# Last group's tail in parts of one, one and two images, bands with tap rows only, first tiles 24 units later

## The reference

```
x = x + L0(gn(x))   # focal modulation: linear, 3 depthwise convs (3, 5, 7), gates, linear, LayerNorm, linear
x = x + L1(gn(x))   # LayerNorm, fp8-quantised MLP 64 -> 512 -> 64
x = x + L2(gn(x))   # circular 7x7 depthwise convs by FFT, gates, 8-step scan, linear
x = x + L3(gn(x))   # deformable 3x3 conv: offsets by a conv, 4-corner gather at 9 taps, linear
```

## Time and profile before

| | |
|---|---|
| median of 3 runs | 5436.56 us (5429.32 to 5450.64) |
| profiled execution | 5432.24 us, its span 5430.4 us |
| mean granted TensorE clock | 0.678 of full speed |
| busy share of DVE, PE, POOL, ACT | 61, 56, 53, 32% |
| bytes moved | 763 MB, mean 141 GB/s |

### The profile page before, as it was taken

The page is one execution under the profiler, slowest core; times in us unless marked ns, Lnnn a source line. Parts: engine busy times, 40 slices in busy tenths (PEclk is TensorE's granted clock), DMA queues, the critical chain, the costliest instruction groups (busy, mean ns, idle before and its releaser), DMA issues. The chain is left out here.

```text
span 5430.4 us, 92964 instructions
## 1 busy us (share of the span) xinstructions
PE 3017.6 (56%) x39574; PEld 2623.4 (48%) x39574; DVE 3303.5 (61%) x4063; ACT 1729.1 (32%) x3209; POOL 2876.9 (53%) x2614
## 2 busy tenths in 40 slices
PE   2873235669644466559744466569744463455333
PEld 2872135559633365449633365469633353444222
DVE  4347843575678755575678765575788655554333
ACT  1223424622234245421233245421333242232000
POOL 1000000465566665565566765674666766677776
PEclk9965655669767666669667666669766666655555
DMA  6841174569633575559633575569633564654333
GB/s 165 169 97 22 29 139 140 145 149 223 149 97 104 127 199 171 146 141 230 140 90 104 135 190 175 155 150 238 141 106 98 149 182 133 178 171 135 109 106 93
DMA packets 776762, 763.09 MB, mean 141 GB/s; under 512 B 575244, under 2 KB 652460, under 8 KB 771916
## 3 DMA queue, kind: packets, MB, share of 16 engines
q1 hardware_dynamic: 651931, 417.24, 33.3%
q0 software_dynamic: 124416, 339.90, 21.7%
HBM read 637.12 MB, written 136.73 MB: 143 GB/s over the span
## 5 line engine op out<-in xcount | busy, mean ns | idle before, releaser
L2129 POOL DMA_INDIRECT e_gb<-corner_table,e_idx x2592 | 2862.3, 1104 | 2534.1 <-DMA e_cws<-cw_all 1084.0
L2191 DVE TENSOR_TENSOR e_vw<-e_gb,e_pc 128x1024 f32<-128x1024 f32 x576 | 774.3, 1372 | 685.4 <-DMA e_gb<-corner_table,e_idx 663.4
L2157 PE MATMUL e_pv<-shifts,e_vw 128*128 128x128 f32 x2744 | 536.7, 365 | 464.0 <-DVE e_vw L2198 463.8
L2157 PEld LDWEIGHTS e_pv<-shifts,e_vw 128*128 128x128 f32 x2744 | 440.3, 190 | 496.9 <-DVE e_vw L2198 474.6
L488 PE MATMUL e_pw<-wk,e_vt 128*64 128x64 f32 (+1 forms) x2880 | 325.1, 285 | 348.0 <-DVE e_xr L2209 221.2
L488 PEld LDWEIGHTS e_pw<-wk,e_vt 128*64 128x64 f32 (+1 forms) x2880 | 279.7, 192 | 410.1 <-issue 248.6
L502 PE MATMUL b_p<-b_x,b_tt 100*100 100x96 f32 x4096 | 398.2, 259 | 32.7 <-DMA b_tt<-zl_copies 32.7
L2167 ACT ACTIVATE e_vt<-e_pv 128x512 f32<-128x512 f32 x288 | 184.2, 640 | 727.3 <-PE e_pw L2157 726.5
L502 PEld LDWEIGHTS b_p<-b_x,b_tt 100*100 100x100 f32 x4096 | 391.0, 176 | 35.3 <-DMA b_tt<-zl_copies 35.2
L1926 ACT ACTIVATE f_xall<-f_p 64x384 f32<-64x384 f32 (+2 forms) x320 | 301.7, 1056 | 132.6 <-PE f_p L1821 130.3
L2198 DVE TENSOR_TENSOR e_vw<-e_vw 128x1152 f32<-128x1152 f32 x233 | 335.4, 1440 | 8.0
(11 more groups left out here) (309 smaller groups left out, 7094.8 us busy)
## 6 DMA issues: line engine op xcount, KB each, us to landing
b_tt<-zl_copies SPq DMA_DIRECT2D x256, 234.0 KB, 9.5
b_tt<-zl_copies SPq DMA_DIRECT2D x128, 390.0 KB
e_gb<-corner_table,e_idx POOLq DMA_INDIRECT x2592
d_px<-x_halo SPq DMA_DIRECT2D x32, 1152.0 KB
corner_table<-f_xn SPq DMA_DIRECT2D x128, 288.0 KB
f_xall<-xpad SPq DMA_DIRECT2D x10, 2400.0 KB, 16.1
x_halo<-d_xo SPq DMA_DIRECT2D x128, 144.0 KB
d_wd<-wd_rows SPq DMA_DIRECT2D x8, 1890.0 KB
```

The source lines that it names most:

```text
L2129: nc.gpsimd.indirect_dma_start(self.gb[k][:, 4 * q:4 * q + 4, :].rearrange("p a c -> p (a c)"), None, T.table[m], off)\
L2157: last = nc.tensor.matmul(dst, vw[:, a, 2 * q:2 * q + nq, :].rearrange("p k c -> p (k c)"), T.ident[:, :], start=(a == 0), stop=(a == n - ...
L2191: v.tensor_tensor(dst, self.gb[k][:, 4 * k0:4 * k1, :].rearrange("p (k a) c -> p k a c", a=4), bc(w, [128, k1 - k0, 4, C], 3), ALU.mult).t ...
```

## The change

- `PARTS`: group 3's D and F run over parts of one, one and two images. `StageF.steps(1)` is a list of its own. Places that took a part of two or more for granted (`load_x(1)`, `k < 2`, `load(0), load(1)`) ask for `P.n`; `P.base // 2` becomes `P.seen[...]`, a count of the images in each buffer; `StageF.act` gets one more place for a tile's copy.
- `StageB.load` brings KS0 rows instead of ND0; `zeros` writes the other rows of both buffers, once a group, on DVE in stage A's step k = 1, p = 0; `first` waits for that.
- `plan`: the first tile is due 24 units after the placement; the third group's spacing (tiles 144 to 215) is made 70/72 of a unit smaller, the last group's is 12.0 instead of 9.0.

```diff
     def load(self, sp, l, q):
         T = self.T
+        n = KS0[l] * PITCH
         for hi in range(2):
-            src = bass.AP(T.zlw.tensor, T.zlw.offset + ORG0[l] - PITCH * hi + 4 * q * W * ZL0,
-                          [[ZL0 - 1, W], [W * ZL0, 4], [1, LB[l]]])
-            dst = halves(self.tt[:, q % 2, OB[l]:OB[l] + 4 * LB[l]])[hi].rearrange("p (c t) -> p c t", c=4)
+            skip = (2 * RD0[l] - KS0[l] // 2 + hi) * PITCH
+            src = bass.AP(T.zlw.tensor, T.zlw.offset + ORG0[l] - PITCH * hi + skip + 4 * q * W * ZL0,
+                          [[ZL0 - 1, W], [W * ZL0, 4], [1, n]])
+            dst = halves(self.tt[:, q % 2, OB[l]:OB[l] + 4 * LB[l]])[hi].rearrange("p (c t) -> p c t", c=4)[:, :, skip:skip + n]
             sp.dma_start(dst, src).then_inc(self.t_in[l][q % 2], 16)
+    def zeros(self, dve, G):
+        for q in range(2):
+            for l in range(3):
+                lead = (2 * RD0[l] - KS0[l] // 2 + 1) * PITCH
+                n = ND0[l] * PITCH - lead - (KS0[l] - 1) * PITCH
+                assert n == lead
+                t = self.tt[:, q, OB[l]:OB[l] + 4 * LB[l]]
+                ap = apv(t, 0, [list(t.ap[0]), [LB[l], 4], [LB[l] - lead, 2], [1, lead]])
+                last = self.nc.vector.memset(ap, 0.0)
+        last.then_inc(self.S.b_zero, 1)
+
     def first(self, sp, G):
         n = 2 * (OB[2] + 4 * LB[2])
+        sp.wait_ge(self.S.b_zero, G + 1)
...
         if k == 1:
             self.st.enter(sp, P.G, P.stage)
-            load_x(1)
+            if P.n > 1:
+                load_x(1)
...
-                pe.wait_ge(self.p_in[m % 2], 48 * (P.base // 2 + m // 2 + 1))
+                pe.wait_ge(self.p_in[m % 2], 48 * (P.seen[m % 2] + m // 2 + 1))
...
     def steps(n):
+        if n == 1:
+            return [10, 14, 6] + [12, 16, 6] + [12, 10, 8] + [1]
         return [10, 14, 6] + [16, 22, 6] + [22, 26, 6] * (n - 2) + [16, 20, 6] + [12, 10, 8] + [1]
...
-PARTS = parts_of([(NI,)] * (NGRP - 1) + [(2, 2)])
+PARTS = parts_of([(NI,)] * (NGRP - 1) + [(1, 1, 2)])
...
-    spaces = [(b - a) / (NI * J) for a, b in zip(starts, starts[1:])] + [9.0]
+    spaces = [(b - a) / (NI * J) for a, b in zip(starts, starts[1:])] + [12.0]
+    spaces[-2] -= 70.0 / (NI * J)
...
                 if tiles == J * loaded:
-                    due = clock
+                    due = clock + 24.0
```

More of the change, by code:

```diff
@@ L672, in dve @@
             gn.dve_var(dve, link, self.psn, PP, i)
+        if k == 1 and p == 0:
+            self.after.zeros(dve, G)
         if 1 <= k <= NI and p:
@@ L697, in __init__ @@
         self.nc, self.T, self.st = nc, T, st
-        self.S = sems(nc, ctx, "b_t00 b_t01 b_t10 b_t11 b_t20 b_t21 b_gap b_zlw b_halo b_c0 b_c1 b_c2 b_g0 b_g1 b_g2 b_acc b_mean b_ctx b_gt")
+        self.S = sems(nc, ctx, "b_t00 b_t01 b_t10 b_t11 b_t20 b_t21 b_gap b_zero b_zlw b_halo b_c0 b_c1 b_c2 b_g0 b_g1 b_g2 b_acc b_mean b_ctx b_gt")
         S = self.S
@@ L1518, in pe @@
             self.st.enter(pe, P.G, P.stage)
-        if k < 2 and p == 0:
+        if k < min(2, P.n) and p == 0:
             gn.pe_sum(pe, self.psn, NH, gn.of(P, 0, k))
@@ L1555, in square @@
         def square():
-            act.wait_ge(self.x_in[k % 2], 64 * (P.base // 2 + k // 2 + 1))
+            act.wait_ge(self.x_in[k % 2], 64 * (P.seen[k % 2] + k // 2 + 1))
             if m >= 1:
@@ L1618, in sums @@
         def sums():
-            dve.wait_ge(self.x_in[k % 2], 64 * (P.base // 2 + k // 2 + 1))
+            dve.wait_ge(self.x_in[k % 2], 64 * (P.seen[k % 2] + k // 2 + 1))
             gn.dve_sums(dve, NH, xs[:, 3:NR + 3, :], self.sq, gn.of(P, 0, k))
@@ L1769, in sp @@
             self.st.enter(sp, P.G, P.stage + 1)
-            load(0)
-            load(1)
+            for m in range(min(2, P.n)):
+                load(m)
             for u in range(2):
@@ L1963, in act @@
             if mid:
+                if not new and not old:
+                    between()
                 moves(0)
@@ L2004, in dve @@
         if p == 1 and j < P.n:
-            dve.wait_ge(self.x_in[j % 2], 16 * (P.base // 2 + j // 2 + 1))
+            dve.wait_ge(self.x_in[j % 2], 16 * (P.seen[j % 2] + j // 2 + 1))
             for g in range(3):
@@ L2209, in result @@
         v.tensor_tensor(xr, xr, self.pso, ALU.add).then_inc(S.e_res, 1)
-Part = namedtuple("Part", "G first n base turn stage")
+Part = namedtuple("Part", "G first n base turn stage seen")
 def parts_of(sizes):
-    parts, turn = [], 0
+    parts, turn, seen = [], 0, (0, 0)
     for G, group in enumerate(sizes):
@@ L2220, in parts_of @@
         for n in group:
-            parts_of_group.append(Part(G, first, n, G * NI + first, turn, 4 + 2 * len(parts_of_group)))
-            first, turn = first + n, turn + 1
+            parts_of_group.append(Part(G, first, n, G * NI + first, turn, 4 + 2 * len(parts_of_group), seen))
+            first, turn, seen = first + n, turn + 1, (seen[0] + (n + 1) // 2, seen[1] + n // 2)
         parts.append(parts_of_group)
     return parts
-PARTS = parts_of([(NI,)] * (NGRP - 1) + [(2, 2)])
+PARTS = parts_of([(NI,)] * (NGRP - 1) + [(1, 1, 2)])
 def sequence():
```

## The result

The changed kernel takes 5380.24 us (5371.95 to 5390.53, 4 runs) beside 5433.0 us for the kernel before: ratio 0.990, interval 0.987 to 0.993, 1.0% faster. A second comparison gave 0.990 again (0.988 to 0.991). The profiled execution has a span of 5388.8 us, 41.6 less than before's.

A forecast was written before the change was run, and what follows sets the result against it. Trunk bounds until image 12's placement, then GpSimd nearly. Placement 4521 - 60 - 20 + 12 - 67 + 13 = 4399; plus 497 + 8 + 439.5 gives span 5343.5, time 5350 us; 8-in-10 range 5280 to 5412.

The forecast's parts named there:

- The stall of the first tile: F's tail after each group's first placement: TensorE's 24.8 us wait goes; -20 us a group, -60 for three.
- Bands: Stage B: loading only tap rows, 15/22 of the bytes, cuts TensorE's waits for bands; -20 us, range 0 to -40.
- The second part: Last group, image 12's placement to image 13's: 84 us to the first gate, then body, F and tiles; 212 us.
- The third part: Last group, images 14 and 15, up to image 14's placement: head 98, bodies 75, F 100, denser tiles 12; 285 us.
- and 12 for the denser tiles: Third part: 12 us added because tiles 12 units apart come every 10.4 us, under GpSimd's 11.7.
- the +66: Image 12's placement to image 14's: second and third parts together take 497 us instead of 431.
- the -31: Image 14's placement to its first tile: GpSimd is idle, so it starts after 7.9 us instead of 38.5.
- seven more tiles in A to L: Last group's stages A to L take seven tiles moved from D and F, 1.9 us each; +13 us, range 0 to +29.
- the head stalls on gathers: Rival: three tiles in each of two heads cost 16.5 us apiece, +99 us, 5450; chance 0.08.
- The moved stall: Rival: tiles 72 to 78 come due at GpSimd's pace, so F's tail ends where it did; +60, 5410; chance 0.15.
- The quick trunk: Rival: parts two and three run at one us a unit (451), F tails gain 29 us each; 5277, chance 0.2.
- the estimate of 5320: Two new heads: at 358 GB/s from HBM their 6.8 MB take 19 us, some 30 us less in all; not adopted.

The follow-up runs named there:

- late48: `parts22` with the first tile due 48 units after the placement instead of 24 and the third group's tiles closer: 5341 us, 0.981 of the kernel before.
- late72: `parts22` with the first tile due 72 units after the placement instead of 24 and the third group's tiles closer: 5316 us, 0.976 of the kernel before.
- space15: The changed kernel with the last group's tiles 15 units apart instead of 12: 5402 us, 0.991 of the kernel before.
- only_late: The kernel before with only the first tile due 24 units after the placement: 5397 us, 0.991 of the kernel before.
- only_bands: The kernel before with only the bands' tap rows loaded, the zeroing memsets and the wait: 5421 us, 0.995 of the kernel before.
- only_parts: The kernel before with only the parts of one, one and two images and their spacings: 5495 us, 1.009 of the kernel before.
- parts22: The changed kernel with the last group's parts and spacings put back to two and two images; bands and 24 units stay: 5374 us, 0.987 of the kernel before.

## Why the prediction was right, and where its steps were off

The direction held, and 5380 us lies in the range, at 0.6 of the gain forecast. Point by point:

- *The stall of the first tile* was right in place and size: 20 us a group forecast, 18, 25 and 12 measured, and -50 us for this edit alone. That GpSimd's pace would be late next was right too: `late48` and `late72` took more from the same stretch.
- *Bands*: right in kind, half the size. The forecast counted TensorE's waits, 33 us, and took 20. Stage B lost 41. What the waits didn't show is the clock, granted at 0.95 for 0.91, and the smaller idle times between the matmuls. The Trainium skill, "DMA: Bandwidth & Descriptors", Anatomy of one DMA, fits a single DMA of the software path as about 2.0 us plus bytes over 436 GB/s. By it a cut band would save an estimated 0.2 us of its landing; the median landing fell by 4.8 us, so the fit doesn't carry over to these transfers of SP's queue, which share the engines at shares of 0.86 to 1.04. Why the granted clock rose wasn't tried.
- *Zeros*: 3.9 us a group forecast, 3.8 measured (16 memsets of 752 ns and 8 of 405).
- *Part one of one image*: -67 forecast, -61.4 measured.
- *The second part* was 212 us in the forecast and is 211, with 83 us from placement to first gate for 84. That is in part luck: 10 of the 83 are waits for gathers that the forecast put at nothing, and with three tiles fewer `space15` took 187, 8 us a tile. *The third part* was 285 and is 313. Its head took 92 us for 98; its bodies and F took 221 for 187.
- The step that failed is "and 12 for the denser tiles": it was mis-sized, and so was the 1.9 us a tile that the forecast took from stages with a tile every 17 us. That VectorE waits 26 us for gathers in the 47 us ahead of image 14's placement doesn't show it, since the kernel before has 27 us there; `space15` does. The forecast saw that 12 units are 10.4 us there, under GpSimd's 11.7, and priced it by the difference. `space15` priced it: 9.7 us a tile. My reading, argued and not tried, is that GpSimd lost 20.5 us with full buffers in the head of part three and then had to make up for it in front of the trunk.
- *The count of tiles* was misread. The prediction has 36 tiles between the placements of images 12 and 14 in both kernels. At 9.0 units a tile, 285 units hold 32, and VectorE's timelines have 216 and 248 tiles weighed at the two placements before, 216 and 252 after. So the +66, and the +92.7 measured, hold four more tiles (39 us at 9.7) as well as one more head, and the -31 behind the placement is the other side of the same four tiles.
- The same mis-sizing stands in "seven more tiles in A to L": +13 forecast, +35 measured in C and L alone. 23 of it are the last group's, with 35 tiles for 30: 4.7 us a tile, not 1.9. C and L of groups 1 and 2 hold 28 tiles before and after and are 6 and 8 us longer; single edits bring as much (6 and 6 us in `only_late`, 3 and 8 in `only_bands`), and why stays open.
- With these prices the parts are a loss: -19 us in the forecast, +26 measured within one chip. That the sum was still right in sign is the work of the other two edits.
- *The idle time* was expected to stand in front of image 14, 60 us; there it is 17.5. Another 64 us lie in gaps between tile 216 and tile 251, 44 of them in the two heads.
- Of the rivals, the head stalls on gathers came in part. The convolution of image 13 waited for its patches, 15.8 us, and not for a tile; but the first gate behind it came 10 us later in the second part's head for gathers, where the rival has six stalls of 16.5 us. The moved stall didn't come. The quick trunk (451 us from image 12 to image 14) is what `space15` reached, 456, but with tiles left over that cost as much behind image 14's placement.
- In the estimate of 5320, 6.8 MB in 19 us and not in 30 (at 228 GB/s) save 11 us a head: 22 for two heads, not 30. The first head moved 221 GB/s here at a DMA share of 0.92, as the sum had it.

Not settled is why the parts alone cost 49 us and with the other edits 26. By the traces most of the difference is in the last group's C and L: 34 us longer than before in `only_parts`, 6.5 us longer in the changed kernel than in `parts22`. Stage B is 14 and 7.5 us longer, and the third group's tail of F 11 and nothing. What makes them so wasn't taken apart.

## What to carry to other kernels

Price a background task by the spacing at which it will run. Here a tile cost the main chain 2 us at a loose spacing, and 9.7 us, near its own engine's 11.7, where that engine was just ahead of the chain. When work is moved so that a starved engine gets its input sooner, ask what it will do until the next input comes; here the two later parts each paid a head of transfers in which GpSimd, with both buffers full, stood still for some of the time. After a long dependency (indices written, loaded, gathered), let the consumers' first wait stand some steps later in every in-order queue, and find the distance by trying it: 24 units gave about half of what 72 did, and 96 no more than 72.

## What the runs showed of the hardware that I had not expected

With a third less to load, stage B ran the same 1686 matmuls at a granted clock of 0.95 to 0.98 for 0.91, and TensorE was busy 150 and 146 us for 158. Over four groups 33 us of short waits for data went and stage B lost 41 and 57 us, more than the waits themselves; whether the clock rose because the waits went wasn't tried apart. A tile's nine indirect gathers took 11.7 us in the last 36 tiles of every trace (11.69 to 11.77), whatever else moved.
